# A graph-network kernel: the copy of the gathered rows goes from ScalarE to Pool, behind Pool's sum of their ends, and the edge stages get a new order

## The chip, the cores and the metric

The kernel runs on one core of one Trainium2 chip. The metric is the device time of one execution in microseconds (us), as the median of the runs shown. A core has five engines with a queue each: PE (TensorE, matrix products; its weight loads are listed as PEld), DVE (VectorE), ACT (ScalarE), POOL (GpSimd) and SP (SyncE, which here only issues transfers). Each works through its own instructions in the order in which they were written; between engines only semaphores order the work.

## The reference, cut to what matters

64 graphs of 128 nodes go through four graph layers, each with a residual and a layer norm. Layers 0 to 2 are dense products with the adjacency matrix. The last one is worked out for each edge:

```python
hi = jnp.einsum('bsh,hk->bsk', x, W1[:H])
hj = jnp.einsum('bsh,hk->bsk', x, W1[H:])
h = jax.nn.relu(hi[:, :, None, :] + hj[:, None, :, :] + b1)
y = _layernorm(jnp.einsum('bijk,kl->bijl', h, W2) + b2, gamma, beta)
out = jnp.einsum('bij,bijh->bih', adj, y)
```

The adjacency matrices are sparse, so the kernel computes `h` only for edges that are there: four slots for each node and a list of at most 256 further edges for each graph.

## The kernel before, in words

Two graphs make a group of 32, and a group of the edge part is called a unit u (q = u mod 2 picks its buffers). Four slots of groups go through the dense layers, staggered, from the start to about 225 us; they leave hi and hj side by side in DRAM (`hh_scratch`, 128 x 512 floats for a unit). From about 185 us on the units of the edge part follow, first mixed with the last dense stages (`passage`), then alone.

For each unit SP loads the 128 x 512 floats into `gH` (`load_h`, L550). A product in a fast form of f32 (the tiles marked f32r) drops low bits, so `gH` is split in two: `split_upper` on ACT (L894 to 899, "spu") copies it with rounding into `gHu`, `split_lower` on POOL (L721 to 727, "spl") subtracts that from `gH` into `gHl`. `add_ends` on POOL (L729 to 733, "hs") adds the two halves of `gH` into `hs`, for edges of a node with itself. PE then gathers the rows of the slots (`gather_ell`, L1585, "g0" and "g1" for the two graphs) and of the list (`gather_csr`, L1604, "gc") out of `gHu`, `gHl` and `hs`.

What follows for a unit: ACT applies the relu ("r0", "r1", "rc", L911 to 921), PE multiplies by W2 ("m0", "m1", "mc", L1621), into banks that ACT has seeded with the bias ("sd0", "sd1", L928), ACT squares ("s0", "s1", L945; "sqc", L951), DVE sums the squares ("d0", "d1", L1264; "dc", L1270), ACT takes the root ("std", L958), DVE the reciprocal ("rec", L1278), POOL multiplies by a mask ("w", L775), DVE weighs the banks ("x0", "x1", L1289; "yn", L1301), and only then can a bank be seeded for the next unit. POOL adds up ("a1", L742; "a2", L749), PE scatters the list ("sc", L1658), DVE adds it ("tot", L1323), POOL applies gamma and the residual ("gm", "rs"), DVE and ACT make the last layer norm ("st", "ag", "om", "fstd", "frec", "sh", "app"). The edges themselves are found by PE ("idx", L1558 and L1560; "rows", L1568; "V", L1575; "cols", L1582), DVE ("T", "Qp", "beg", "T2") and ACT ("kS", "kST").

The order of the work on each engine is written out by hand. `T3` gives each stage a moment, `PERIOD3 / 2` = 8.3 is the step from unit to unit, and `flow` (L453) sorts an engine's stages by their moment within two steps; the whole steps in a moment tell by how many units the stage lags. The numbers set an order alone: no engine waits for a time. `passage` (L464) does the same for the first eight units, mixed with the last dense stages, with moments of their own in `FIRST`. `units` (L481) then runs a loop whose turn has two units, and writes the last ones out behind the loop. The SP stage `next_h` (L203) loads the `gH` of two units on; it waits for `split_done` and `hs_ready`.

```python
times = [(moment(when) + PERIOD3 / 2 * q, i, q) for i, (when, _) in enumerate(stages) for q in K2]
for at, i, q in sorted((at % PERIOD3, i, q) for at, i, q in times):
    age = int((moment(stages[i][0]) + PERIOD3 / 2 * q) // PERIOD3)
    if age in ages:
        stages[i][1](q, 2 * (p - age) + q, lambda d=0: counts(q - 2 * age - d))
```

Of the kernel before, what the change touches and what calls it, by code (L numbers as in the profile page):

```python
# [39 lines left out]
def gnn_stack(nc, x_d, a_d, at_d, mask_d, diag_d, front_d, back_d, eps_d, a_g, at_g, out_d):  # L40
# [17 lines left out]
    with ctx:  # L58
# [276 lines left out]
        def count(r):  # L335
            return [SLOTS * r + k + 1 for k in K4]
# [24 lines left out]
        def wait_past(engine, semaphore, n):  # L361

            if not isinstance(n, int) or n > 0:
                engine.wait_ge(semaphore, n)  # L364
# [3 lines left out]
        T3 = {"idx": 18.98, "rows": 29.95, "V": 33.91, "cols": 36.46, "g0": 34.64, "g1": 38.22, "gc": 38.09, "m0": 38.25, "m1": 38.57, "mc": 38.29,  # L368
# [4 lines left out]
        AGES = 4  # L373
        START3, EARLY, CATCH = 216.0, 5.0, 25.0
        FIRST = {("Qp", 0): 219.13, ("Qp", 1): 221.26, ("Qp", 2): 230.17, ("Qp", 3): 240.76, ("Qp", 4): 250.69, ("Qp", 5): 261.11, ("Qp", 6): 305.61,
# [7 lines left out]
                 ("app", 0): 261.65, ("app", 1): 287.96, ("app", 2): 294.07, ("app", 3): 370.14, ("app", 4): 384.7, ("app", 5): 423.77,  # L383
                 ("app", 6): 430.26, ("app", 7): 449, ("beg", 0): 220.26, ("beg", 1): 224.6, ("beg", 2): 226.72, ("beg", 3): 247.12,
                 ("beg", 4): 260.14, ("beg", 5): 296.17, ("beg", 6): 305.17, ("beg", 7): 434.92, ("cols", 0): 224.14, ("cols", 1): 230.68,
                 ("cols", 2): 239.99, ("cols", 3): 258.69, ("cols", 4): 258.91, ("cols", 5): 260.34, ("cols", 6): 278.16, ("cols", 7): 338.69,
# [4 lines left out]
                 ("frec", 3): 354.98, ("frec", 4): 377.23, ("frec", 5): 433.5, ("frec", 6): 479.84, ("frec", 7): 597.74, ("fstd", 0): 255.59,  # L391
                 ("fstd", 1): 272.03, ("fstd", 2): 304, ("fstd", 3): 307.1, ("fstd", 4): 329.45, ("fstd", 5): 360.71, ("fstd", 6): 387.64,
# [6 lines left out]
                 ("idx", 0): 211.57, ("idx", 1): 218.85, ("idx", 2): 223.6, ("idx", 3): 233.78, ("idx", 4): 236.94, ("idx", 5): 258.03,  # L399
                 ("idx", 6): 286.2, ("idx", 7): 350.18, ("kS", 0): 221.2, ("kS", 1): 226.38, ("kS", 2): 233.39, ("kS", 3): 246, ("kS", 4): 260.44,  # L400
                 ("kS", 5): 276.11, ("kS", 6): 286.16, ("kS", 7): 439.02, ("kST", 0): 224.68, ("kST", 1): 231.7, ("kST", 2): 244.22,
                 ("kST", 3): 257.09, ("kST", 4): 272.39, ("kST", 5): 277.83, ("kST", 6): 309.45, ("kST", 7): 322.08, ("m0", 0): 218.58,
# [8 lines left out]
                 ("rec", 0): 230.93, ("rec", 1): 243.38, ("rec", 2): 253.14, ("rec", 3): 266.15, ("rec", 4): 286.69, ("rec", 5): 371.3,  # L411
                 ("rec", 6): 380.43, ("rec", 7): 395.56, ("rows", 0): 220.19, ("rows", 1): 225.18, ("rows", 2): 231.18, ("rows", 3): 252.04,
                 ("rows", 4): 273.75, ("rows", 5): 312.4, ("rows", 6): 322.8, ("rows", 7): 347.8, ("rs", 0): 239.21, ("rs", 1): 252.36,
# [1340 lines left out]
```

## Time and profile before

| | us |
|---|---|
| median of 3 runs | 449.18 |
| lowest and highest run | 448.45, 449.66 |
| the profiled execution's own time | 449.61 |
| its span, first to last instruction | 447.9 |

The profiled execution is 0.43 us above the median; 1.7 us of it lie outside the span. In the rows, times are in us from the start of the span, durations in us (in the lists of groups the mean is in ns). A matmul's end is modelled, so a row of PE can be longer than the time after which the next one starts; what a stage takes of PE is read from start to start.

### The profile page before, as it was taken

To read this page: it belongs to the slowest core of one execution; us is meant where nothing else is said; L and a number is where in the kernel's file an instruction comes from. 1 tells how busy PE (TensorE), PEld (TensorE's weight loads), DVE (VectorE), ACT (ScalarE), POOL (GpSimd) and SP (SyncE) were. 2 spreads that over 40 slices of the span, in tenths; PEclk is the share of its full clock that TensorE was granted. 3 is DMA by queue.
4 is the path that set the end of the run, shared out by engine and by line. 5 is a ranking of instruction groups with operands and counts; after the bars stand their busy time and mean duration, and the time that the engine had idled before them with its cause. 6 is when DMAs were issued, how large, how long until landed. Compare 5 with 4: busy or idle time off the path is not lost. (4 is left out here: it accounts for less than half of the span.)

```text
span 447.9 us, 14059 instructions
## 1 busy us (share of the span) xinstructions
PE 429.5 (96%) x3391; PEld 403.8 (90%) x3391; DVE 422.7 (94%) x1555; ACT 393.8 (88%) x1001; POOL 353.6 (79%) x651
## 2 busy tenths in 40 slices
PE   7599989999999999999999999999999999999993
PEld 3599989999999999898999999999999999999992
DVE  6999999999999999998999999999999999999976
ACT  2378979999999899979899999999999999999994
POOL 3569979999999899953776878787878787878772
PEclk9989999999999999999999999999999999999998
DMA  6134334445444743232422223222323232323111
GB/s 225 43 86 124 101 127 159 154 157 159 155 157 152 240 162 120 80 129 78 136 89 73 88 66 92 66 92 64 94 64 94 64 94 63 95 65 97 59 37 50
DMA packets 50939, 47.60 MB, mean 106 GB/s; under 512 B 5584, under 2 KB 42576, under 8 KB 50896
## 3 DMA queue, kind: packets, MB, share of 16 engines
q1 hardware_dynamic: 49760, 46.45, 33.7%
q10 hardware_dynamic: 1136, 0.66, 0.5%
q8 instruction: 16, 0.26, 0.2%
q14 instruction: 27, 0.22, 0.2%
HBM read 28.22 MB, written 18.87 MB: 105 GB/s over the span
## 5 line engine op out<-in xcount | busy, mean ns | idle before, releaser
L1621 PE MATMUL bank<-w2c,hE 128*128 128x128 f32 x512 | 68.3, 277 | 0.4 <-ACT bank L928 0.4
L1621 PEld LDWEIGHTS bank<-w2c,hE 128*128 128x128 f32 x512 | 63.5, 192 | 2.6 <-issue 0.7
L1289 DVE TENSOR_TENSOR ym<-bank,wE 128x512 f32<-128x512 f32 x64 | 43.4, 684 | 4.3 <-POOL wE L775 3.3
L1264 DVE TENSOR_REDUCE ssum<-sqE 128x4 f32<-128x512 f32 x63 | 42.7, 678 | 3.0 <-ACT sqE L945 2.7
L1122 DVE BATCH_NORM_STATS2 stats<-t 128x6 f32<-128x128 f32 x192 | 44.5, 273 | 1.0 <-issue 1.0
L945 ACT ACTIVATE sqE<-bank 128x512 f32<-128x512 f32 x63 | 38.0, 603 | 8.0 <-PE bank L1621 8.0
L915 ACT ACTIVATE hE<-bank,front 128x512 f32<-128x512 f32 x64 | 43.5, 680 | 1.5 <-PE bank L1601 1.5
L742 POOL TENSOR_TENSOR half<-ym 128x512 f32<-128x512 f32 x31 | 39.6, 1276 | 5.7 <-DVE ym L1289 2.1
L775 POOL TENSOR_TENSOR wE<-erstd,fits 128x12 f32<-128x12 f32 x31 | 6.6, 213 | 44.8 <-DVE erstd L1278 44.8
L726 POOL TENSOR_TENSOR gHl<-gH,gHu 128x512 fp32r<-128x512 f32 x32 | 40.8, 1276 | 1.2 <-ACT gHu L899 1.2
L928 ACT ACTIVATE bank<-b2c 128x512 f32<-128x512 f32 x62 | 37.4, 604 | 0.5 <-DVE ym L1289 0.4
L1621 PEld LDWEIGHTS bank<-w2c,hC 128*128 128x128 f32 x256 | 33.6, 191 | 2.3
L838 ACT ACTIVATE std<-mv,eps_col 128x2 f32<-128x2 f32 x96 | 25.2, 294 | 11.0 <-DVE mv L1129 10.5
L1658 PE MATMUL bank<-yC,ST 128*128 128x128 f32 x256 | 34.1, 276 | 0.1
L1461 PE MATMUL bank<-back,xT 128*128 128x128 f32 x256 | 33.8, 275 | 0.0
L1621 PE MATMUL bank<-w2c,hC 128*128 128x128 f32 x256 | 33.7, 275 | 0.0
L1461 PE MATMUL bank<-back,x3T 128*128 128x256 f32 x128 | 33.1, 381 | 0.0
L1658 PEld LDWEIGHTS bank<-yC,ST 128*128 128x128 f32 x256 | 31.1, 192 | 1.0 <-ACT yC L965 0.6
L1461 PEld LDWEIGHTS bank<-back,xT 128*128 128x128 f32 x256 | 31.1, 192 | 0.4
L1239 DVE TENSOR_TENSOR TE<-bank,odd 128x768 fp32r<-128x768 f32 x32 | 30.1, 942 | 0.4 <-PE bank L1560 0.4
L1139 DVE TENSOR_SCALAR x<-t,mv,rstd 128x128 f32<-128x128 f32 x64 | 29.8, 506 | 0.0
L665 POOL TENSOR_TENSOR A<-A,scaled_id 128x256 f32<-128x256 f32 x32 | 23.5, 735 | 7.5 <-DMA A<-adj_groups 6.4
(192 smaller groups left out, 1643.6 us busy)
## 6 DMA issues: line engine op xcount, KB each, us to landing
hh_scratch<-hh SPq DMA_DIRECT2D x32, 256.0 KB, 2.2
gH<-hh_scratch SPq DMA_DIRECT2D x32, 256.0 KB, 2.7
A<-adj_groups SPq DMA_DIRECT2D x32, 128.0 KB, 2.1
res_scratch<-res SPq DMA_DIRECT2D x32, 128.0 KB, 2.0
gRES<-res_scratch SPq DMA_DIRECT2D x32, 128.0 KB, 2.0
AT<-adjT_groups SPq DMA_DIRECT2D x31, 128.0 KB, 2.2
out<-y SPq DMA_DIRECT2D x30, 128.0 KB, 1.8
X<-x_groups SPq DMA_DIRECT2D x29, 128.0 KB, 2.2
```

The source lines that it names most:

```text
L726: nc.gpsimd.tensor_tensor(run(gHl[q][:, :, :]), run(gH[q][:, :, :]), run(gHu[q][:, :, :]).bitcast(f32), ALU.subtract).then_inc(b["split_do ...
L742: nc.gpsimd.tensor_tensor(half[:, :, :, :], ym[q][:, :, 0:2, :], ym[q][:, :, 2:4, :], ALU.add).then_inc(b["half_done"], 1)
L915: nc.scalar.activation(hE[g][:, :], HE_ps, ACT.Relu, bias=C["L3_b1"]).then_inc(b[f"hE{g}_ready"], 1)
L928: nc.scalar.activation(YE_ps[g], b2c[:, :].unsqueeze(1).to_broadcast([P, ELL, P]), ACT.Copy).then_inc(b[f"seedE{g}_done"], 1)
L945: nc.scalar.activation(sqE[g][:, :, :], YE_ps[g], ACT.Square).then_inc(b[f"sqE{g}_ready"], 1)
L1122: last = nc.vector.bn_stats(stats[layer][k][:, g, :], t[layer][k][:, g, :])
L1239: nc.vector.tensor_tensor(TE[q][:, :, :, :], QT_ps.unsqueeze(2).to_broadcast([P, GROUP, ELL - 1, P]), odd[:, :, :].unsqueeze(1).to_broadca ...
L1264: nc.vector.tensor_reduce(ssum[q][:, g * ELL:(g + 1) * ELL], sqE[g][:, :, :], AX.X, ALU.add).then_inc(b[f"ssE{g}_ready"], 1)
L1289: nc.vector.tensor_tensor(ym[q][:, g, :, :], YE_ps[g], spread_last(wE[q][:, g * ELL:(g + 1) * ELL]), ALU.mult).then_inc(b[f"ymE{g}_ready"], 1)
L1461: last = nc.tensor.matmul(out[:, g, :], lhs(g), rhs(g), start=bias is None, stop=bias is None or g == GROUP - 1)
L1621: last = nc.tensor.matmul(ps[:, i, :], hidden[:, i * P:(i + 1) * P], w2c[:, :], start=False, stop=i == tiles - 1, skip_group_check=seeded)
L1658: last = nc.tensor.matmul(O_ps[:, g, :], ST[q][:, g * CSR + c, :], yC[q][:, g * CSR + c, :], start=c == 0, stop=c == CSR - 1)
```

## The change

POOL in place of ACT writes `gHu`: the copy stands in `add_ends`, right behind the sum, and `add_ends` also waits for what `split_upper` waited for. ACT loses the stage. `next_h` gets its moment from "spl" alone. All of `T3` and `FIRST` have new numbers. The arithmetic, the tiles, the buffers and the number of transfers stay as they are.

```diff
-        T3 = {"idx": 18.98, "rows": 29.95, "V": 33.91, "cols": 36.46, "g0": 34.64, "g1": 38.22, "gc": 38.09, "m0": 38.25, "m1": 38.57, "mc": 38.29,
-              "sc": 49.97, "spu": 17.7, "kS": 20.33, "kST": 26.68, "r0": 26.25, "r1": 27.55, "rc": 27.48, "sd0": 26.7, "sd1": 28.48, "s0": 28.66,
...
+        T3 = {"idx": 4.94, "rows": 17.75, "V": 20.35, "cols": 21.39, "g0": 21.09, "g1": 23.66, "gc": 26.08, "m0": 26.84, "m1": 28.97, "mc": 28.75,
+              "sc": 38.3, "kS": 17.04, "kST": 20.91, "r0": 20.1, "r1": 25.96, "rc": 25.46, "sd0": 21.63, "sd1": 26.73, "s0": 26.77, "s1": 28.28,
...
-            edge_stages = [(("idx", 0.5), next_ot), (("spl", "hs", 1.5), next_h), (("rs", 0.8), next_res), (("app", 1), store)]
+            edge_stages = [(("idx", 0.5), next_ot), (("spl", 1.5), next_h), (("rs", 0.8), next_res), (("app", 1), store)]
...
                 wait_past(pool, b["HE1_psum"], count(2))
+                wait_past(pool, b["HC_psum"], count(2))
                 nc.gpsimd.tensor_tensor(hs[q][:, :, :], gH[q][:, :, 0:P], gH[q][:, :, P:2 * P], ALU.add).then_inc(b["hs_ready"], 1)
+                nc.gpsimd.tensor_copy(gHu[q][:, :, :], gH[q][:, :, :]).then_inc(b["split_up"], 1)
...
-            def split_upper(q, u, count):
-
-                act.wait_ge(gh_loaded[q], (u - q) * 8 + 16)
-                wait_past(act, b["HE1_psum"], count(2))
-                wait_past(act, b["HC_psum"], count(2))
-                nc.scalar.activation(gHu[q][:, :, :], gH[q][:, :, :], ACT.Copy).then_inc(b["split_up"], 1)
-
...
-            edge_stages = [("spu", split_upper), ("kS", keep_S), ("kST", keep_ST), ("r0", hidden_ell(0)),
+            edge_stages = [("kS", keep_S), ("kST", keep_ST), ("r0", hidden_ell(0)),
```

Sorted by the two tables, each engine goes round in these orders, one round for each unit. The number behind a stage is its whole steps of 8.3: a stage with a larger one works on an earlier unit.

```
before PE   sc6 V4 g0-4 idx2 cols4 gc4 g1-4 m0-4 rows3 mc4 m1-4   (every second round rows before m0)
after  PE   rows2 gc3 m0-3 V2 mc3 m1-3 g0-2 cols2 idx0 sc4 g1-2
before DVE  yn5 T2 st6 ag6 Qp2 d0-4 dc4 d1-4 T2-3 rec4 tot5 frec6 x0-4 beg2 x1-4
after  DVE  Qp1 st5 T2-2 ag5 d0-3 dc3 d1-3 beg1 rec3 tot4 x0-3 frec5 yn3 T0 x1-3
before ACT  spu2 r0-3 kST3 sd0-3 rc3 r1-3 sd1-3 kS2 s0-3 sqc3 s1-3 fstd5 app6 std3
after  ACT  kS2 rc3 r1-3 sd1-3 s0-3 sqc3 fstd5 s1-3 r0-2 std3 kST2 app6 sd0-2
before POOL hs3 a2-5 w4 gm5 om6 sh6 rs5 a1-4 spl2
after  POOL w4 hs2 (and the copy) gm5 rs5 om6 spl2 sh6 a1-4 a2-4
```

The loop's turn begins on ACT with "spu" of an even unit before and with "kS" after; on PE with "sc" before and "rows" after.

## Rows read from the trace of the kernel before

**Rows 1.** The page, busy time and share of the span of each engine

```profile
PE 429.5 (96%) x3391; PEld 403.8 (90%) x3391; DVE 422.7 (94%) x1555; ACT 393.8 (88%) x1001; POOL 353.6 (79%) x651
```

**Rows 2.** Timeline of PE, 303 to 318: start, us, engine, line, operation, tiles, count

```profile
303.19 0.48 PE L1575 MATMUL bank<-S,Qp 128*128 128x256 f32 x2
...
303.51 0.34 PE L1597 MATMUL bank<-TE,gHu 128*128 128x384 f32 x1
...
304.76 0.36 PE L1611 MATMUL bank<-S,gHu 128*128 128x256 f32 x1
...
305.79 0.34 PE L1597 MATMUL bank<-TE,gHu 128*128 128x384 f32 x1
...
306.82 1.05 PE L1621 MATMUL bank<-w2c,hE 128*128 128x128 f32 x8
...
307.71 0.38 PE L1619 MATMUL bank<-bias,ones_b 128*128 128x512 bf16 x1
...
308.81 1.06 PE L1621 MATMUL bank<-w2c,hE 128*128 128x128 f32 x8
...
309.71 1.06 PE L1658 MATMUL bank<-yC,ST 128*128 128x128 f32 x8
...
310.52 0.48 PE L1575 MATMUL bank<-S,Qp 128*128 128x256 f32 x2
...
313.33 0.41 PE L1597 MATMUL bank<-TE,gHu 128*128 128x384 f32 x1
...
318.20 0.48 PE L1575 MATMUL bank<-S,Qp 128*128 128x256 f32 x2
```

**Rows 3.** Timeline of PE behind the loop: the stage "V", two units apart

```profile
407.91 0.48 PE L1575 MATMUL bank<-S,Qp 128*128 128x256 f32 x2
...
422.57 0.48 PE L1575 MATMUL bank<-S,Qp 128*128 128x256 f32 x2
```

**Rows 4.** Timeline of ACT, DVE and POOL in the loop, 302 to 313

```profile
302.58 0.60 ACT L945 ACTIVATE sqE<-bank 128x512 f32<-128x512 f32 x1 [0.29 <-PE bank L1621]
...
303.21 0.69 DVE L1264 TENSOR_REDUCE ssum<-sqE 128x4 f32<-128x512 f32 x1
...
303.26 0.87 ACT L987 ACTIVATE y<-tout,oshift,orstd 128x128 f32<-128x128 f32 x2
...
304.03 0.29 ACT L958 ACTIVATE esd<-ssum,eps_col 128x12 f32<-128x12 f32 x1
...
304.41 0.22 DVE L1278 RECIPROCAL erstd<-esd 128x12 f32<-128x12 f32 x1
...
304.82 0.21 POOL L775 TENSOR_TENSOR wE<-erstd,fits 128x12 f32<-128x12 f32 x1 [1.34 <-DVE erstd L1278]
...
305.06 0.69 DVE L1289 TENSOR_TENSOR ym<-bank,wE 128x512 f32<-128x512 f32 x1
...
311.87 0.63 ACT L899 ACTIVATE gHu<-gH 128x512 fp32r<-128x512 f32 x1 [0.18 <-issue]
...
312.41 0.67 ACT L915 ACTIVATE hE<-bank,front 128x512 f32<-128x512 f32 x1
```

**Rows 5.** Timeline of DVE: "rec", once for each unit, at three moments

```profile
205.37 0.23 DVE L1278 RECIPROCAL erstd<-esd 128x12 f32<-128x12 f32 x1
...
244.35 0.22 DVE L1278 RECIPROCAL erstd<-esd 128x12 f32<-128x12 f32 x1
...
423.79 0.22 DVE L1278 RECIPROCAL erstd<-esd 128x12 f32<-128x12 f32 x1
```

**Rows 6.** Groups of POOL's instructions, whole span: busy us, mean ns, idle before

```profile
L742 POOL TENSOR_TENSOR half<-ym 128x512 f32<-128x512 f32 x31 | 39.6, 1276 | 5.7 <-DVE ym L1289 2.1 <-issue 0.5
...
L733 POOL TENSOR_TENSOR hs<-gH 128x256 f32<-128x256 f32 x32 | 23.3, 729 | 0.0
...
L640 POOL TENSOR_SCALAR_AFFINE_SELECT ident<-ident 128x128 f32<-128x128 f32 x1 | 0.3, 292 | 0.2 <-POOL ident L638 0.2
```

**Rows 7.** The page, DMA issues: size, us from issue to landing

```profile
gH<-hh_scratch SPq DMA_DIRECT2D x32, 256.0 KB, 2.7
```

More of the change, by code:

```diff
@@ L364, in wait_past @@
                 engine.wait_ge(semaphore, n)
-        T3 = {"idx": 18.98, "rows": 29.95, "V": 33.91, "cols": 36.46, "g0": 34.64, "g1": 38.22, "gc": 38.09, "m0": 38.25, "m1": 38.57, "mc": 38.29,
[4 rows of a table removed]
+        T3 = {"idx": 4.94, "rows": 17.75, "V": 20.35, "cols": 21.39, "g0": 21.09, "g1": 23.66, "gc": 26.08, "m0": 26.84, "m1": 28.97, "mc": 28.75,
[4 rows of a table added]
         AGES = 4
         START3, EARLY, CATCH = 216.0, 5.0, 25.0
-        FIRST = {("Qp", 0): 219.13, ("Qp", 1): 221.26, ("Qp", 2): 230.17, ("Qp", 3): 240.76, ("Qp", 4): 250.69, ("Qp", 5): 261.11, ("Qp", 6): 305.61,
[7 rows of a table removed]
[L383 to L386, printed above, removed]
[4 rows of a table removed]
-                 ("frec", 3): 354.98, ("frec", 4): 377.23, ("frec", 5): 433.5, ("frec", 6): 479.84, ("frec", 7): 597.74, ("fstd", 0): 255.59,
-                 ("fstd", 1): 272.03, ("fstd", 2): 304, ("fstd", 3): 307.1, ("fstd", 4): 329.45, ("fstd", 5): 360.71, ("fstd", 6): 387.64,
[6 rows of a table removed]
[L399 to L402, printed above, removed]
[8 rows of a table removed]
-                 ("rec", 0): 230.93, ("rec", 1): 243.38, ("rec", 2): 253.14, ("rec", 3): 266.15, ("rec", 4): 286.69, ("rec", 5): 371.3,
-                 ("rec", 6): 380.43, ("rec", 7): 395.56, ("rows", 0): 220.19, ("rows", 1): 225.18, ("rows", 2): 231.18, ("rows", 3): 252.04,
-                 ("rows", 4): 273.75, ("rows", 5): 312.4, ("rows", 6): 322.8, ("rows", 7): 347.8, ("rs", 0): 239.21, ("rs", 1): 252.36,
[8 rows of a table removed]
-                 ("sh", 7): 368.47, ("spl", 0): 212.77, ("spl", 1): 218.79, ("spl", 2): 225.48, ("spl", 3): 235.56, ("spl", 4): 245.46,
-                 ("spl", 5): 259.39, ("spl", 6): 312.86, ("spl", 7): 374, ("spu", 0): 183.55, ("spu", 1): 217.3, ("spu", 2): 226.04,
-                 ("spu", 3): 232.29, ("spu", 4): 244.95, ("spu", 5): 254.16, ("spu", 6): 270.1, ("spu", 7): 284.7, ("sqc", 0): 228.99,
-                 ("sqc", 1): 236.21, ("sqc", 2): 245.83, ("sqc", 3): 259.45, ("sqc", 4): 276.27, ("sqc", 5): 277.67, ("sqc", 6): 292.79,
-                 ("sqc", 7): 376.85, ("st", 0): 249.46, ("st", 1): 262.52, ("st", 2): 275.92, ("st", 3): 336.82, ("st", 4): 372.9, ("st", 5): 374.49,
-                 ("st", 6): 400.55, ("st", 7): 412.66, ("std", 0): 231.68, ("std", 1): 239.35, ("std", 2): 251.61, ("std", 3): 264.53,
-                 ("std", 4): 314.04, ("std", 5): 322.9, ("std", 6): 327.82, ("std", 7): 334.05, ("tot", 0): 245.11, ("tot", 1): 254.06,
-                 ("tot", 2): 265.45, ("tot", 3): 271.56, ("tot", 4): 320.85, ("tot", 5): 338.09, ("tot", 6): 360.32, ("tot", 7): 453.47,
[5 rows of a table removed]
@@ new lines, in gnn_stack @@
+        FIRST = {("Qp", 0): 220.15, ("Qp", 1): 222.18, ("Qp", 2): 227.92, ("Qp", 3): 232.97, ("Qp", 4): 243.03, ("Qp", 5): 266.69, ("Qp", 6): 272.02,
[7 rows of a table added]
+                 ("app", 0): 270.64, ("app", 1): 272.75, ("app", 2): 311.63, ("app", 3): 319.35, ("app", 4): 324, ("app", 5): 337.17,
+                 ("app", 6): 343.76, ("app", 7): 344.78, ("beg", 0): 218.93, ("beg", 1): 220.35, ("beg", 2): 226.15, ("beg", 3): 238.33,
+                 ("beg", 4): 249.78, ("beg", 5): 256.22, ("beg", 6): 272.56, ("beg", 7): 301.65, ("cols", 0): 224.14, ("cols", 1): 228.98,
+                 ("cols", 2): 236.08, ("cols", 3): 246.69, ("cols", 4): 256.31, ("cols", 5): 271.7, ("cols", 6): 304.66, ("cols", 7): 319.18,
[4 rows of a table added]
+                 ("frec", 3): 288.08, ("frec", 4): 300.78, ("frec", 5): 308.43, ("frec", 6): 334.76, ("frec", 7): 348.64, ("fstd", 0): 264.45,
+                 ("fstd", 1): 269.3, ("fstd", 2): 284.54, ("fstd", 3): 299.62, ("fstd", 4): 299.88, ("fstd", 5): 312.29, ("fstd", 6): 331.32,
[6 rows of a table added]
+                 ("idx", 1): 219.73, ("idx", 2): 224.2, ("idx", 3): 229.51, ("idx", 4): 237.02, ("idx", 5): 245.79, ("idx", 6): 263.51,
+                 ("idx", 7): 277.23, ("kS", 0): 220.16, ("kS", 1): 225.21, ("kS", 2): 230.13, ("kS", 3): 247.28, ("kS", 4): 254.31,
+                 ("kS", 5): 268.23, ("kS", 6): 274.55, ("kS", 7): 277.38, ("kST", 0): 224.13, ("kST", 1): 229.51, ("kST", 2): 244.38,
+                 ("kST", 3): 250.86, ("kST", 4): 264.82, ("kST", 5): 273.51, ("kST", 6): 286.82, ("kST", 7): 289.84, ("m0", 0): 214,
[8 rows of a table added]
+                 ("rec", 1): 238.92, ("rec", 2): 245.98, ("rec", 3): 265.54, ("rec", 4): 277.29, ("rec", 5): 280.95, ("rec", 6): 293.82,
+                 ("rec", 7): 353.11, ("rows", 0): 218.44, ("rows", 1): 225.68, ("rows", 2): 229.97, ("rows", 3): 245.54, ("rows", 4): 250.89,
[9 rows of a table added]
+                 ("spl", 0): 212.39, ("spl", 1): 220.14, ("spl", 2): 231.35, ("spl", 3): 238.57, ("spl", 4): 255.13, ("spl", 5): 267.81,
+                 ("spl", 6): 274.76, ("spl", 7): 301.16, ("sqc", 0): 228.75, ("sqc", 1): 235.42, ("sqc", 2): 244.58, ("sqc", 3): 261.58,
+                 ("sqc", 4): 270.35, ("sqc", 5): 287.93, ("sqc", 6): 301.45, ("sqc", 7): 315.46, ("st", 0): 262.53, ("st", 1): 269.11,
+                 ("st", 2): 277.79, ("st", 3): 282.33, ("st", 4): 286.63, ("st", 5): 291.99, ("st", 6): 295.86, ("st", 7): 311.73,
+                 ("std", 0): 229.65, ("std", 1): 236.07, ("std", 2): 248.56, ("std", 3): 262.39, ("std", 4): 272.35, ("std", 5): 283.9,
+                 ("std", 6): 285.9, ("std", 7): 290.72, ("tot", 0): 245.72, ("tot", 1): 249.79, ("tot", 2): 266.23, ("tot", 3): 277.06,
+                 ("tot", 4): 306.49, ("tot", 5): 311.99, ("tot", 6): 331.3, ("tot", 7): 340.57, ("w", 0): 231.72, ("w", 1): 240.81, ("w", 2): 253.75,
[5 rows of a table added]
```

83 rows, old and new, of tables (FIRST, T3) are left out of this document.

## The prediction, as it was put on record

> **What bounds the kernel now.** I read the page's busy shares first. PE, DVE and ACT stand at 96, 94 and 88%, POOL at 79% [rows 1]: three engines are nearly full, so the shares don't tell which of them sets the pace. The timeline of the edge part does. In the loop the stage "V" of PE starts at 303.19, 310.52 and 318.20, after 7.33 and then 7.68 us [rows 2]. In the 7.33 us round PE has no hole. Read from start to start, V takes 0.32, g0 with idx and cols 1.25, gc 1.03, g1 and rows 1.03, m0 0.89, mc 1.10, m1 0.90, sc 0.81 (309.71 to 310.52); together 7.33. Behind the loop the rounds take (422.57 - 407.91) / 2 = 7.33 each [rows 3]. So 7.33 us is what PE needs for a unit, and only the 0.35 us more in every second round is anybody's waiting.
>
> That waiting begins on ACT. ACT's square of m1 waits 0.29 us for PE, and from there ACT runs back to back to the next "spu", which in the longer round stands 0.18 us late with no other engine to wait for ("issue": the turn of the loop) [rows 4]. The relu r0 behind it ends at 312.41 + 0.67 = 313.08, and PE's g1, which needs it, starts at 313.33 with a matmul of 0.41 us where the other round has 0.34 [rows 2, 4]. ACT's order is so full that a slip of 0.18 us reaches PE, and PE's seeds come as late.
>
> From rec at 244.35 to rec at 423.79 are 24 units, 7.477 us each; from 205.37 to 244.35, where dense and edge work mix, five units of 7.80 [rows 5].
>
> **The change, part by part.** *ACT* loses 32 copies. One takes 0.54 us of it from start to start (311.87 to 312.41) [rows 4], 17 us in all, but none of it was on PE's path except through the slip. What it can give back is PE's waiting: 7.477 - 7.33 = 0.15 us for a unit in the steady part, and up to 5 x (7.80 - 7.33) = 2.3 us before it.
>
> *POOL* gains a copy of 512 elements, which the trace of before does not have on this engine. The sum of two inputs of that size takes 1.276 us, that of 256 elements 0.729 [rows 6], so 2.14 ns for an element of a two-input operation and 0.18 us beside. The one-input row, a select over 128 elements, takes 0.292 [rows 6]: with the same 0.18 beside, 0.9 ns an element. At that slope the copy takes 0.18 + 512 x 0.9 = 0.63 us, at the other 1.28. These are my ends. I take 0.7, since a copy has one input as the select has.
>
> The Trainium skill's "GPSIMD Engine Reference", section "Engine selection", speaks against this change in its first half: elementwise work of two inputs is about twice as slow there as on VectorE; in its second half one-input work is called roughly line-rate. By the first half the sum would come out as in the first rival below, by the second as in my forecast. No run here shows which holds for a copy.
>
> Does POOL keep up? I put the clock at 0 when PE leaves m1 of unit u; in the rows that is 308.81 + 0.90 = 309.71 in one round, and 7.33 us earlier, 302.38, in the round that I read now. The square starts 0.20 after it (302.58), d1 at 0.83, std at 1.65, rec at 2.03, w at 2.44, x0 at 2.68 [rows 4]. In the new order POOL goes from w to hs, copy, gm, rs, om and spl, which PE's g0 of two units on awaits. With the rows of the same size (0.73 for hs, gm and rs, 0.21 for w and om, 1.28 for spl) spl ends at 2.44 + 0.21 + 3 x 0.73 + 0.21 + 1.28 + C = 6.33 + C, C being the copy [rows 4, 6]. PE wants it at 7.33, so C may be 1.0; at 0.7 there are 0.3 us to spare. POOL's whole round is 6.1 + C = 6.8 us, under 7.33.
>
> *The new order* must close its loop in one round: m1 of u, square, d1, std, rec, w, x0, seed sd0, m0 of u+1, V, mc, m1. x0 ends at 2.68 + 0.69 = 3.37. On ACT std, kST and app stand before sd0. std starts no sooner than 1.65; std's 0.29, kST's 0.6 (the square's size) and app's 0.87 [rows 4], each starting up to 0.1 before the last one ends, free ACT at about 3.2, so the seed runs from 3.4 to 4.0 (the seed has the size of the square, 0.60). PE meanwhile does g0, cols and idx, sc, g1 and rows, gc: 1.25 + 0.81 + 1.03 + 1.03 = 4.12 [rows 2]. The seed is there 0.1 us before, and the loop closes in 4.0 + 0.06 + 0.89 + 0.32 + 1.10 + 0.90 = 7.27, just under PE's 7.33. tot stands between rec and x0 and needs sc, which leaves PE at 1.25 + 0.81 = 2.06; starting 0.2 later, with half of x0's elements and so about half of its 0.69 us, it is over at about 2.6, before x0 at 2.68. The order thus fits PE's pace but with little to spare, and I take 7.36.
>
> *Waits and transfers.* "hs" now also waits for gc of two units back, which left PE more than 5 us before; the wait is free, and behind it on POOL only gm would be late. spl no longer waits for another engine. `next_h` is issued when spl is over; the load lands 2.7 us later [rows 7] and is used by hs in about two rounds less the 4 us between hs and spl: some 8 us to spare. On SP it stands behind the store and next_res, whose waits come within the round. The turn of the loop on ACT now falls between the seed and kS, where V wants kS about half a microsecond after its end: covered. The drain keeps its stages behind the last m1, so I give it nothing.
>
> *Sum.* Steady part: 24 x (7.477 - 7.36) = 2.8 us less. Mixed part: half of 2.3 us, since ACT's copies are one cause of several there: 1.1 us less. Against the profiled execution's own 449.61 us that is 445.7; it stood 0.43 above the median, so against 449.18 I say 445.3 us.
>
> **The rivals.** *The copy costs what a two-input operation costs.* With C = 1.28 spl ends at 7.61 and g0 of unit u+2 waits. From w of u over that g0 to w of u+2 are two rounds: 6.33 + 1.28 - 2.44, then PE's round of 7.33, then 2.44, together 14.94, so 7.47 a round, today's 7.48. The gain is gone: about 449 us. For it: every large POOL row has two inputs and that price [rows 6]; against: the one-input row has not.
>
> *The seed comes late, and the kernel is slower.* The loop over m1, rec, w, x0 and sd0 crosses engines eight times and has 0.06 us to spare. If the crossings take 0.3 us more together than in the rows (w, now in front of hs and the copy on a fuller POOL, or sd0 behind app), m0 waits and each round takes 7.27 + 0.3 = 7.57: 24 x 0.09 = 2.2 us more, 451.4. It decides from 0.2 us on. For it: eight crossings read from another order; against: each is a row of this kernel, and their durations hardly vary.
>
> *The mixed part gets worse.* POOL gets copies there while it also does dense work, and the order of `FIRST` is all new. If the five units took 8.2 us in place of 7.8, 2 us would be lost instead of 1.1 gained, and the time would be 448.4: no change that can be told.
>
> *More than I say.* If PE's waiting went altogether, in both parts, 24 x 0.147 + 2.3 = 5.8 us: 443.4.
>
> **How the numbers follow.** A measurement of this kernel tells 0.3%, 1.35 us, from no change. My forecast, with what lies between it and the last case, has 0.62; the two-input copy 0.15; the late seed 0.14; the worse mixed part 0.09. The late seed is slower, and so are, I think, 0.02 of the copy's case and 0.03 of the mixed one's, where the losses add to what the order costs: 0.19. The rest of those two, 0.19, is no change. Faster is 0.62. The range must reach from the case with no waiting left, with 2 us below it for waits in the dense part and at the end that I have not counted, 441.3, to the late seed's 451.4; leaving out the outer parts of both, I say 441.5 to 451.
>
> **What would show it.** Right: rounds of 7.3 to 7.4 us without the pair of 7.33 and 7.68; POOL's copy at 0.6 to 1.0 us and the engine near 90% busy in the edge part; ACT with several tenths of idle time a round, most before its squares and rc; PE's g1 without a late matmul. Wrong: a copy near 1.28 us with g0 waiting for spl (the first rival); m0 starting right behind the end of sd0 in every round (the second); longer rounds before 245 us than now (the third).

## The result, and the profile after

The changed kernel takes 457.05 us (455.67 to 457.98, four runs) against 449.06 for the kernel before beside it: a ratio of 1.0175, 95% interval 1.0145 to 1.0205. It is slower by 8.0 us where I forecast 3.9 faster, and outside my range. The profiled execution is 457.98, its span 456.2, 8.4 us more than before's.

The page of the changed kernel, busy time of each engine (answers to [rows 1]):

```profile
PE 435.4 (95%) x3358; PEld 405.0 (89%) x3391; DVE 422.3 (93%) x1555; ACT 383.2 (84%) x969; POOL 370.0 (81%) x683
```

ACT lost 10.6 us of work and POOL gained 16.4: the copy is where it was meant to be. POOL's groups give its price (busy us, mean ns, idle before; they answer to [rows 6]):

```profile
L725 POOL TENSOR_TENSOR gHl<-gH,gHu 128x512 fp32r<-128x512 f32 x32 | 41.0, 1281 | 0.0
...
L733 POOL TENSOR_TENSOR hs<-gH 128x256 f32<-128x256 f32 x32 | 23.4, 731 | 1.0 <-PE bank L1608 1.0
...
L734 POOL CAST gHu<-gH 128x512 fp32r<-128x512 f32 x32 | 19.8, 617 | 0.0
```

A copy takes 0.617 us, just under the lower of my two bounds (0.63), so its price isn't what costs. Where the time went is read from "rec", once for each unit, in DVE's timeline (answers to [rows 5]):

```profile
206.77 0.23 DVE L1272 RECIPROCAL erstd<-esd 128x12 f32<-128x12 f32 x1 [0.45 <-ACT esd L952]
...
247.59 0.22 DVE L1272 RECIPROCAL erstd<-esd 128x12 f32<-128x12 f32 x1
...
431.84 0.22 DVE L1272 RECIPROCAL erstd<-esd 128x12 f32<-128x12 f32 x1
```

The 24 units behind 247.59 take (431.84 - 247.59) / 24 = 7.677 us each, before 7.477: 4.8 us. The five units ahead of them take 40.82, before 38.98: 1.8 us. The first rec comes 1.4 us later; over this kernel and those below that keep its order it falls anywhere from 203.67 to 206.77, so that I give this part no cause. The last two units take 0.3 us more, and from the last rec to the end it is 9.92 us in both.

In the loop all rounds are now alike, 7.68 us. PE, ACT, DVE and POOL in one of them, from g0 of a unit to the next g0 (timeline; answers to [rows 2] and [rows 4]):

```profile
306.80 0.42 PE L1591 MATMUL bank<-TE,gHu 128*128 128x384 f32 x1
307.08 0.60 ACT L939 ACTIVATE sqE<-bank 128x512 f32<-128x512 f32 x1
...
308.14 1.11 PE L1652 MATMUL bank<-yC,ST 128*128 128x128 f32 x8
308.49 0.30 ACT L952 ACTIVATE esd<-ssum,eps_col 128x12 f32<-128x12 f32 x1
308.84 0.22 DVE L1272 RECIPROCAL erstd<-esd 128x12 f32<-128x12 f32 x1
309.00 0.42 PE L1591 MATMUL bank<-TE,gHu 128*128 128x384 f32 x1
309.25 0.21 POOL L776 TENSOR_TENSOR wE<-erstd,fits 128x12 f32<-128x12 f32 x1 [0.79 <-DVE erstd L1272]
309.29 0.42 DVE L1317 TENSOR_TENSOR tot<-bank,accE 128x256 f32<-128x256 f32 x1 [0.23 <-PE bank L1652]
309.34 0.60 ACT L903 ACTIVATE ST<-bank 128x512 f32<-128x512 f32 x1 [0.55 <-PE bank L1652]
...
309.62 0.68 DVE L1283 TENSOR_TENSOR ym<-bank,wE 128x512 f32<-128x512 f32 x1
309.84 0.86 ACT L981 ACTIVATE y<-tout,oshift,orstd 128x128 f32<-128x128 f32 x2
...
310.09 0.38 PE L1562 MATMUL bank<-begun,diff 128*128 128x512 bf16 x1
...
310.61 0.58 ACT L922 ACTIVATE bank<-b2c 128x512 f32<-128x512 f32 x1
...
311.34 1.13 PE L1615 MATMUL bank<-w2c,hE 128*128 128x128 f32 x8
...
314.48 0.43 PE L1591 MATMUL bank<-TE,gHu 128*128 128x384 f32 x1
```

The reader is to see the bracket behind ACT's L903, the stage kST. It has stood still for 0.55 us until PE finished "sc" (L1652), and behind it on ACT come app and the seed sd0 (L922), on which PE's m0 (L1615, 311.34) starts 0.15 us after its end. kST writes the buffer `ST[q]`, which sc of two units back still reads; the line `wait_past(act, b["O_psum"], count(2))` in `keep_ST` says so.

PE meets the late kST twice. m0 waits for the seed behind it. Ahead of m0, "rows" (L1562, `start_rows`) waits for kST itself, in the line `wait_past(pe, b["ST_ready"], count(1))`: kST reads the PSUM bank that rows writes. It starts at 310.09, 0.15 us after kST's end. The list of waits from 250 to 400 us (engine, line, releaser: us in total, times, longest) has kST's wait in every round, and PE's at rows (where "issue" names no releaser, the next row names kST):

```profile
ACT ST L903 <- PE bank L1652: 10.6, 19, 0.6
DVE tot L1317 <- PE bank L1652: 4.4, 19, 0.2
...
PEld bank L1562 <- issue: 2.7, 9, 0.3
PEld bank L1562 <- ACT ST L903: 2.4, 10, 0.2
```

In the kernel before, none of these waits is in the list.

### The profile page after: what moved, and what is told of

Read it like the earlier page. It is cut to its first block and busy times, and to the rows that moved or that the text cites. A ratio compares the mean times of both kernels' runs of the same rounds, so it can differ in the third digit from the quotient of the medians.

```text
span 456.2 us, 14007 instructions
## 1 busy us (share of the span) xinstructions
PE 435.4 (95%) x3358; PEld 405.0 (89%) x3391; DVE 422.3 (93%) x1555; ACT 383.2 (84%) x969; POOL 370.0 (81%) x683
## 5 line engine op out<-in xcount | busy, mean ns | idle before, releaser
L1615 PE MATMUL bank<-w2c,hE 128*128 128x128 f32 x512 | 69.2, 279 | 1.2 <-ACT hE L909 0.6
L1615 PEld LDWEIGHTS bank<-w2c,hE 128*128 128x128 f32 x512 | 62.2, 191 | 4.1 <-issue 1.1
L922 ACT ACTIVATE bank<-b2c 128x512 f32<-128x512 f32 x62 | 36.9, 598 | 0.5 <-DVE ym L1283 0.5
L1652 PE MATMUL bank<-yC,ST 128*128 128x128 f32 x256 | 35.5, 282 | 0.7 <-ACT hh L879 0.4
L1615 PE MATMUL bank<-w2c,hC 128*128 128x128 f32 x256 | 33.7, 275 | 2.1
L1615 PEld LDWEIGHTS bank<-w2c,hC 128*128 128x128 f32 x256 | 33.9, 193 | 0.9
L1652 PEld LDWEIGHTS bank<-yC,ST 128*128 128x128 f32 x256 | 31.1, 192 | 1.7 <-ACT yC L959 0.6
L903 ACT ACTIVATE ST<-bank 128x512 f32<-128x512 f32 x32 | 19.1, 596 | 14.3 <-PE bank L1652 14.3
L718 POOL TENSOR_TENSOR res<-x,sums 128x256 f32<-128x256 f32 x32 | 22.2, 694 | 9.7 <-DMA hh_scratch<-hh 4.8
```

The source lines that it names most:

```text
L922: nc.scalar.activation(YE_ps[g], b2c[:, :].unsqueeze(1).to_broadcast([P, ELL, P]), ACT.Copy).then_inc(b[f"seedE{g}_done"], 1)
L1615: last = nc.tensor.matmul(ps[:, i, :], hidden[:, i * P:(i + 1) * P], w2c[:, :], start=False, stop=i == tiles - 1, skip_group_check=seeded)
L1652: last = nc.tensor.matmul(O_ps[:, g, :], ST[q][:, g * CSR + c, :], yC[q][:, g * CSR + c, :], start=c == 0, stop=c == CSR - 1)
```

## The experiments

Times are medians; a ratio is to the kernel before, run beside it. "Round" is the mean over the 24 units from the sixth rec to the thirtieth, "mixed" the time from the first rec to the sixth (before: 7.477 and 38.98).

### sc ahead of cols

```diff
-              "sc": 38.3, "kS": 17.04,
+              "sc": 37.9, "kS": 17.04,
```

> The kernel after, with one moment changed: sc stands before cols and idx on PE in place of behind them. Theory (kST waits for sc): in the kernel after, kST starts 0.3 us behind the end of sc and stands 0.55 us idle for it, and app, the seed sd0, and PE's rows come behind kST. With sc some 0.4 us earlier kST starts when cols is done, the seed is there before m0, and a round takes 7.33 to 7.4 us in place of 7.69: some 8 us less than after, near 449 to 450. Rival (POOL's fuller round sets the pace): sc has no part in it, the round stays at 7.69, 457. Rival (many crossings, each a little late): a part of it, 7.55 to 7.65.

451.23 us, ratio 1.0029 (1.0005 to 1.0052); round 7.459, mixed 40.83. One number takes some 6 us off, 24 x (7.677 - 7.459) = 5.2 of them in the loop. It puts sc ahead of idx, too. ACT and PE in a round of it, timeline:

```profile
320.29 1.06 PE L1652 MATMUL bank<-yC,ST 128*128 128x128 f32 x8
...
321.61 0.60 ACT L903 ACTIVATE ST<-bank 128x512 f32<-128x512 f32 x1 [0.22 <-PE bank L1576]
...
322.10 0.86 ACT L981 ACTIVATE y<-tout,oshift,orstd 128x128 f32<-128x128 f32 x2
...
322.96 0.60 ACT L922 ACTIVATE bank<-b2c 128x512 f32<-128x512 f32 x1
...
323.71 1.13 PE L1615 MATMUL bank<-w2c,hE 128*128 128x128 f32 x8
```

kST now waits 0.22 us, for cols, which leaves PE behind sc, and PE's wait at rows is gone from the list. The rounds alternate between 7.33 and 7.63, and m0 still starts 0.15 us after the seed's end: something further holds this loop.

### app ahead of kST

```diff
-              ... "app": 54.72, ...            (("app", 1), store)
+              ... "app": 54.03, ...            (("app", 1.69), store)
```

> The kernel after, with app moved in front of kST on ACT, into the hole in which kST waits for sc. Theory: the seed sd0 no longer stands behind the whole wait and is in time for m0; but rows on PE still waits for kST, which ends as late as now, so only the part of PE's wait at m0 goes: a round of 7.5 to 7.65 us, 453 to 456. POOL theory: no change, 7.69 and 457. If the seed alone were the cause: 7.33 to 7.4, 449 to 450.

454.4 us, ratio 1.0115 (1.0076 to 1.0154); round 7.610. A third of the steady loss goes, as expected. Timeline of ACT and PE, and the list of waits:

```profile
328.86 0.57 ACT L903 ACTIVATE ST<-bank 128x512 f32<-128x512 f32 x1
...
329.49 0.39 PE L1562 MATMUL bank<-begun,diff 128*128 128x512 bf16 x1
...
329.80 0.60 ACT L922 ACTIVATE bank<-b2c 128x512 f32<-128x512 f32 x1 [0.37 <-DVE ym L1283]
...
330.72 1.05 PE L1615 MATMUL bank<-w2c,hE 128*128 128x128 f32 x8
```

```profile
PEld bank L1562 <- issue: 4.0, 10, 0.4
...
PEld bank L1562 <- ACT ST L903: 3.4, 10, 0.3
```

The seed is over at 330.40, 0.32 before m0, so that m0 no longer waits for it: that wait was worth 0.07 us a round. What is left is PE's wait at rows for kST, which now stands behind app. So the changed kernel's loop has two waits behind kST, and an earlier sc shortens both.

### The old order with POOL's copy

`split_upper` leaves ACT; "hs" and the copy stand right ahead of "spl" on POOL, the rest keeps the order of before.

```diff
-              "spl": 23.72, "hs": 25.25, ...
+              "spl": 23.72, "hs": 23.7, ...
+                nc.gpsimd.tensor_copy(gHu[q][:, :, :], gH[q][:, :, :]).then_inc(b["split_up"], 1)
```

> The kernel before with its old order, where only hs, and the copy behind it, stand right in front of spl on POOL and the copy is gone from ACT: the change without the new order. Theory: the copy itself costs 0.61 us of POOL, which has the time, and frees 0.54 us of ACT, whose slip at the turn of the loop then no longer reaches PE: rounds of 7.33 to 7.42 us in place of 7.50, and 444 to 447 us, faster than both. POOL theory: POOL's chain holds PE and rounds take 7.6 us or more, 452 or more.

456.46 us, ratio 1.014 (1.0098 to 1.0182); round 7.57, mixed 42.55. The theory missed and its rival held. PE waits in every second round ahead of g0 (L1592), which needs spl, the last of a POOL chain that is now two instructions longer; in one such round spl ends at 340.53 and g0's weights load at 340.73. In the list of waits:

```profile
PEld bank L1592 <- issue: 2.8, 9, 0.3
```

### The new order with ACT's copy

The changed kernel, the copy back on ACT between std and kST.

```diff
+              "spu": 12.55, "kS": 17.04, ...
-                nc.gpsimd.tensor_copy(gHu[q][:, :, :], gH[q][:, :, :]).then_inc(b["split_up"], 1)
```

> The kernel after with its new order, but the copy back on ACT, between std and kST, where ACT waits for sc anyway: the new order without the new engine. Theory: the copy fills the hole of 0.55 us, the round stays at 7.69 and the time at 456 to 458. POOL theory: POOL is relieved by 0.6 us and the round goes back to 7.5 or less, 452 or less.

457.9 us, ratio 1.0194 (1.0156 to 1.0232); round 7.679, mixed 41.34. The changed kernel has 7.677: which engine copies makes no difference to it, because ACT does the copy in the time in which it waits for sc, as its timeline shows:

```profile
331.36 0.30 ACT L959 ACTIVATE esd<-ssum,eps_col 128x12 f32<-128x12 f32 x1
331.56 0.61 ACT L900 ACTIVATE gHu<-gH 128x512 fp32r<-128x512 f32 x1
332.22 0.60 ACT L910 ACTIVATE ST<-bank 128x512 f32<-128x512 f32 x1
```

kST starts 2.55 us after g0 (329.67), in the changed kernel 2.54. The loss in the steady part is the new order's, not the copy's.

### The old order, copy ahead of a1

As the third, with "a1" behind spl on POOL (40.1 to 41.0), so that spl is out of PE's way, and "hs" of the first two units at its moment of before.

> As the run with the copy alone in the old order, but on POOL a1 moves from in front of hs, copy and spl to behind spl; in the mixed part hs and copy of the first two units stand as early as hs stood before. In that other run PE's g0 waited for spl in both rounds, since hs and copy (1.3 us) stand in POOL's chain from w to spl. Theory (the copy costs nothing where it isn't in the chain that PE waits for): without a1 (1.28 us) the chain is as short as before, PE's g0 no longer waits for spl and the steady rounds are 7.33 to 7.40 us; with the mixed part still as long as there, 446 to 453 in all. Rival (POOL's whole round is too full, whatever its order): rounds stay at 7.60.

452.95 us, ratio 1.0079 (1.0058 to 1.01); mixed 41.53, round 7.476: the pair of 7.42 and 7.59 stands just as it stood before. ACT has no copy in it, so the slip ahead of the copy, from which my prediction had all the waiting begin, is gone with it, and the round has not changed. The place to look is w. Timeline of DVE and POOL, two rounds of this kernel:

```profile
327.84 0.22 DVE L1273 RECIPROCAL erstd<-esd 128x12 f32<-128x12 f32 x1
...
328.42 0.21 POOL L777 TENSOR_TENSOR wE<-erstd,fits 128x12 f32<-128x12 f32 x1 [0.75 <-DVE erstd L1273]
...
335.43 0.22 DVE L1273 RECIPROCAL erstd<-esd 128x12 f32<-128x12 f32 x1
...
335.84 0.21 POOL L777 TENSOR_TENSOR wE<-erstd,fits 128x12 f32<-128x12 f32 x1 [0.70 <-DVE erstd L1273]
```

w starts 0.58 us after rec in one round and 0.41 in the other, and x0, the seed and m0 follow it. The kernel before has the same two, 0.57 and 0.41; its [rows 4] show the shorter. The trace also records what POOL's sequencer (it takes the waits and the register instructions) does, though no view lists it: in the kernel before it leaves the wait for rec 0.25 us after rec's start; in the shorter round one register instruction (the address of the unit's mask in `fits`) stands between that and w; in the longer one there are an addition and another wait ahead of it, since the thresholds of the waits written behind the one for rec are worked out only then.

### beg and Qp exchanged

The first experiment with DVE's "Qp" and "beg" in each other's place (9.14 and 10.95), to free rec of beg, which stands right ahead of it.

> The new order with sc early, and on DVE beg and Qp change places, so that rec stands behind 0.34 us of work after d1 and not behind 0.65. With sc early PE still waits at m0 in each round for the seed sd0, which comes behind m1, square, d1, beg, rec, w, x0. Theory (that loop closes in 7.48): rec starts some 0.1 us sooner, the seed too, and a round takes 7.35 to 7.42, 24 x 0.1 = 2 us less than with sc early alone. Rival (the rest of the wait is not that loop): 7.48 as before, no change.

463.93 us, ratio 1.0308 (1.0287 to 1.0329). It tells nothing about beg, since PE then waits in "idx" (L1552) for the later Qp (list of waits):

```profile
PEld bank L1552 <- DVE Qp L1242: 8.8, 10, 0.9
```

### The wait for rec last

In `weights` the wait for rec goes behind the three others, all of which were over long before.

```diff
-                pool.wait_ge(b["erstd_ready"], count())
                 wait_past(pool, b["ymE0_ready"], count(2))
                 wait_past(pool, b["ymE1_ready"], count(2))
                 wait_past(pool, b["yC_ready"], count(2))
+                pool.wait_ge(b["erstd_ready"], count())
```

In the kernel before:

> The kernel before, with one edit: in the stage "w" the wait for rec comes last of its four waits instead of first. In the trace of before, POOL's sequencer comes out of that wait 0.25 us after rec starts and only then works out what the other waits and the address of the mask need, so that w starts 0.41 us after rec in one round and 0.57 in the next. Theory A (the waiting of the kernel before sits in this hop of w, not on ACT): w starts about 0.30 us after rec in every round, the pair of 7.41 and 7.60 falls to 7.33 to 7.40, and the time falls by 24 x 0.12 = 2 to 3.5 us, to about 446. Rival B (my prediction's premise: the waiting begins with ACT's slip of 0.18 us at the turn of its loop): w starts earlier, but the rounds stay at 7.41 and 7.60 and the time at 449.

449.33 us, ratio 0.9991 (0.9977 to 1.0005). Two rounds, DVE and POOL:

```profile
326.43 0.22 DVE L1278 RECIPROCAL erstd<-esd 128x12 f32<-128x12 f32 x1
...
326.83 0.21 POOL L775 TENSOR_TENSOR wE<-erstd,fits 128x12 f32<-128x12 f32 x1 [1.31 <-DVE erstd L1278]
...
334.02 0.22 DVE L1278 RECIPROCAL erstd<-esd 128x12 f32<-128x12 f32 x1
...
334.43 0.21 POOL L775 TENSOR_TENSOR wE<-erstd,fits 128x12 f32<-128x12 f32 x1 [1.51 <-DVE erstd L1278]
```

w now starts 0.40 and 0.41 after rec, and the rounds are still 7.41 and 7.59. ACT's slip is still in the list of waits (ahead of L899, 1.8 us in 10 times, as before). By itself this speaks for ACT's slip, as the fifth experiment by itself speaks against it.

In the fifth experiment's kernel, where ACT has no copy:

> The old order with POOL's copy ahead of a1 (the run with the copy before a1), and the same edit of w's waits. ACT has no copy here. Theory A: rounds of 7.33 to 7.40 instead of 7.42 and 7.59, the mixed part unchanged at 41.5, so about 450 us against its 452.95 without the edit. Rival B would have had this kernel at 7.33 without the edit and expects no further change.

451.41 us, ratio 1.0037 (1.002 to 1.0054); mixed 42.39, and the pair is gone: 7.42 and 7.43, a mean of 7.408. So two waits of the same length stand side by side in the kernel before, w's late start and one on ACT; taking away either is worth nothing, both 0.07 us a round. That the one on ACT is the slip and not the copy's own time is argued, not shown: these kernels lose both together, and have a1 in another place on POOL.

The mixed part of a single profile can be off by about 1 us: here it is 42.39 against 41.53 in the fifth experiment, whose profiled execution was 2.2 us under its median, while the same edit of w changed it little elsewhere (38.98 to 38.90 in the kernel before, 40.83 to 40.67 in the run that follows).

In the first experiment's kernel:

> The changed kernel with sc ahead of cols (first experiment) and the same edit of w's waits. If its loop m1, s1, d1, std, rec, w, x0, sd0, m0 is what still keeps PE waiting, the edit takes 0.1 us out of one round and 0.28 out of the next, and the rounds fall from 7.33 and 7.63 to 7.33 to 7.36 each: 24 x 0.12 = 3 us off 451.2, about 448.3. If something else holds PE (the seed behind app, or T behind the register work of beg), the rounds stay near 7.46 and the time near 451.

449.95 us, ratio 1.0005 (0.9987 to 1.0022); round 7.395 (7.33 and 7.48), half of the gain expected. With two edits, one number and one line, the changed kernel is level with the kernel before.

### ACT copies in the mixed part, POOL in the loop

The order and `FIRST` of before; ACT copies for the units of `passage`, POOL in the loop and behind it, in the order of the fifth experiment; rec's wait last.

```diff
+            units(pool, [(n, add_ends_and_copy if n == "hs" else f) for n, f in edge_stages], counted=(0, 1))
+            units(act, [x for x in edge_stages if x[0] != "spu"])
```

> The kernel before with its FIRST and ACT's copy kept in the mixed part; in the loop and behind it POOL copies (order of the run with the copy before a1), and w's wait for rec comes last of its waits. Theory: two waits stood side by side in the kernel before, w's hop and ACT's slip behind its copy, and the mixed part lost only where POOL copied in it. Then rec 0 to 5 takes 39.0 us as before, the rounds 7.42, and the time is 24 x 0.07 = 1.6 us under before: about 448, ratio 0.996 to 0.997. If the mixed part's loss came from the order that the loop needs and not from POOL's copies, rec 0 to 5 stays at 41.5 or more and the time at 450 to 451.

448.62 us, ratio 0.9986 (0.9966 to 1.0006); round 7.406, mixed 39.35. Its first and sixth rec, and then those of the kernel with the same edits that lets POOL copy in the mixed part, too (DVE's timeline):

```profile
205.64 0.23 DVE L1286 RECIPROCAL erstd<-esd 128x12 f32<-128x12 f32 x1
...
244.99 0.22 DVE L1286 RECIPROCAL erstd<-esd 128x12 f32<-128x12 f32 x1
```

```profile
205.60 0.23 DVE L1273 RECIPROCAL erstd<-esd 128x12 f32<-128x12 f32 x1
...
248.00 0.22 DVE L1273 RECIPROCAL erstd<-esd 128x12 f32<-128x12 f32 x1
```

The two differ in who copies for the first units, and in the moments of "hs" there (and with them of next_h), since POOL's sum stands in front of its copy: 3.0 us together (2.8 between the medians, 451.41 and 448.62). The timeline shows where. With POOL's copies the engine works without a stop from w of the second unit (213.84) to w of the third (224.06), with two sums and two copies in between, 2.7 us, that the other kernel has not there; that w starts 1.77 us after its rec, in the other 0.38.

### The mask fetched ahead of the wait

POOL takes the unit's mask into a small tile ahead of its waits, so that w has no address to work out; the wait for rec stays last.

```diff
+                nc.gpsimd.tensor_tensor(fitq[q][:, :], zeros[:, 0:ROWS3], fits[:, bass.ds(u, 1), :].rearrange("p o d -> p (o d)"), ALU.add).then_inc(b["fit_ready"], 1)
...
-                nc.gpsimd.tensor_tensor(wE[q][:, :], erstd[q][:, :], fits[:, bass.ds(u, 1), :].rearrange("p o d -> p (o d)"), ALU.mult).then_inc(b["wE_ready"], 1)
+                nc.gpsimd.tensor_tensor(wE[q][:, :], erstd[q][:, :], fitq[q][:, :], ALU.mult).then_inc(b["wE_ready"], 1)
```

In the kernel just described:

> The same, and POOL takes the unit's mask into a small tile ahead of its wait for rec (one more POOL instruction of 12 elements, about 0.21 us, in time in which POOL waits), so that w itself has no address to work out behind the wait. Theory (0.10 us of the 0.40 between rec and w is the address): w starts 0.30 us after rec, as behind the loop, rounds of 7.33 to 7.36 instead of 7.42, 24 x 0.08 = 1.9 us less than the run without it: about 446, ratio 0.992. Rival: the 0.09 us by which 7.42 stands over 7.33 is another wait, and the rounds stay at 7.42.

447.37 us, ratio 0.995 (0.9931 to 0.9969), the one kernel here that beats both. Its rec and w, timeline:

```profile
244.14 0.21 DVE L1290 RECIPROCAL erstd<-esd 128x12 f32<-128x12 f32 x1
...
324.94 0.22 DVE L1290 RECIPROCAL erstd<-esd 128x12 f32<-128x12 f32 x1
...
325.30 0.21 POOL L787 TENSOR_TENSOR wE<-erstd,fitq 128x12 f32<-128x12 f32 x1
...
420.40 0.22 DVE L1290 RECIPROCAL erstd<-esd 128x12 f32<-128x12 f32 x1
```

The hop is 0.36, not the 0.30 expected, and the round (420.40 - 244.14) / 24 = 7.344: PE's own 7.33 but for 0.01.

In the changed kernel with sc ahead of cols:

> The changed kernel with sc ahead of cols and the mask taken ahead of the wait, w's wait for rec last. Theory: rounds of 7.33 to 7.36 in place of 7.33 and 7.48, 1.2 us less than with the waits alone in another order: about 448.7, ratio 0.998. Rival: the longer round waits for something that no edit of w reaches (the seed behind app, or the begun stage ahead of rec), and the rounds stay at 7.33 and 7.48.

449.32 us, ratio 0.9993 (0.9976 to 1.001); round 7.354, mixed 41.20. Its steady part is now under my forecast of 7.36, and what it had gained there, 24 x (7.477 - 7.354) = 3.0 us, the mixed part takes back for the most part (2.2 us).

## Why the prediction was wrong

**PE needs 7.33 us for a unit, whatever the order: right.** The mean rounds of 7.344 and 7.354 of the last two kernels come within 0.03 of it in both orders, and none is below it.

**The copy at 0.7, POOL keeps up: right.** It took 0.617; the first rival is out, and in the loop of the changed kernel PE's list of waits has no row for spl. Of the two halves of the rule in the Trainium skill's "GPSIMD Engine Reference", "Engine selection", that I had set against each other, this trace agrees with the first: the subtraction of 128x512, with two inputs, takes 1.281 us where DVE's product of that size, with two, takes 0.68 (309.62 above). It doesn't speak against the second: the copy costs about what ACT needed for it (0.63, [rows 4]), and no copy of this size runs on DVE here.

**The new order's loop closes in 7.27: this is the step that failed, and the main loss (4.8 of the 8 us).** In that step I let kST start as soon as std was over and had ACT free at 3.2 on a clock that starts when PE leaves m1. In the rows of after that moment is 306.80. sc leaves PE at 309.00, 2.20 on that clock (I had 2.06); kST, waiting for it, starts at 2.54; the seed runs from 3.81 to 4.39 where I had 3.4 to 4.0; m0 starts at 4.54 where I had 4.12. From m0 to the end of m1 it takes 3.14 (I had 3.21), and the round is 7.68. I had seen that tot needs sc and priced that; that kST does, too, stands in the same function that I had costed by its duration, and I did not read its waits. Nor did I read those of rows, which waits for kST: I had g1 and rows at 1.03, and here they take 309.00 to 310.21, 1.21 (gc stands at 310.21). Moving sc gave back 0.22 us a round: shown. Of that the seed's lateness alone is 0.07, as the second experiment shows; the rest went with PE's wait at rows. The second rival named one of the two places (m0 behind the seed) at 7.57, but had its price from the crossings.

**The crossings: too short as well.** I took w at 0.41 after rec from one round of a loop whose turn has two; the other round has 0.57, and in the changed kernel 0.58. In the changed kernel itself this costs nothing yet, since its rounds are 7.68 behind either hop; it shows once sc is early. From the first experiment to the last the round falls from 7.459 to 7.354, by edits of w's waits and address alone: 0.10 us a round that the sum had at nothing.

**"That waiting begins on ACT": half of it.** A wait on ACT, by my reading the slip, and w's hop kept PE waiting side by side. I followed the chain back to the first cause that explained the longer round and stopped.

**The mixed part: forecast 1.1 us of gain, measured 1.8 of loss.** My third rival, "the mixed part gets worse", was right, at about its price (2 us). In the old order POOL's copies there, with the sums moved in front of them, cost 3.0 us: shown, though not which of the two. In the new order they are not the cause, or not the only one, since the mixed part is 41.34 with ACT's copy, at the moments that I gave it, against 40.82. That leaves the new `FIRST`, by elimination: the old `FIRST` under the new loop was not run, so which of its moments costs stays open, and so do the 1.4 us ahead of the first rec.

**The drain at nothing, next_h with time to spare: right.** From the last rec to the end nothing changed, and no wait for `gH` appears in the loop. That the new wait of hs for gc is free holds in the loop alone: in the mixed part hs stood 0.66 and 0.38 us for it, the 1.0 in POOL's row L733 above. What that cost no run here tells.

## What to carry to other kernels

When a stage moves, read every wait in its function, those for a buffer's reuse too, and ask for each where its releaser now stands in the new order; a stage costed by its duration alone hides them. In a loop whose turn has two units read both rounds, and before you call one wait the cause, ask whether another of the same length stands beside it: then each alone tests as worth nothing. In such a loop put the wait that ends last behind the others, and its instruction's address work ahead of it: the two together gave 0.10 us a round here.

## What the runs showed that I had not expected

Register work of an engine's sequencer shows in the time from one engine to the next. From the start of rec to the start of w, the same 12 elements take 0.56 to 0.60 us with a threshold and an address still to be worked out behind the wait, 0.40 to 0.42 with the address alone, and 0.36 with neither. Behind the loop, where these are constants, it is 0.30 with rec's wait first and, to my surprise, 0.39 with rec's wait last. The records of POOL's sequencer show where the two differ. With rec's wait first, w's own instruction holds that wait. With rec's wait last, an instruction of its own holds it and begins 0.25 us after rec's start; w, which now holds another wait, begins 0.14 later. The kernels with the mask first have such an instruction in the loop, too (0.25, and w 0.11 behind it), where I had expected 0.30.
